# Cross-attention stage of a Perceiver layer on one core: score groups in pairs, Strassen's blocks in three PSUM banks, C22 summed into SBUF

## The chip, the core and the metric

The kernel runs on one core of one Trainium2 chip. The metric is the device time of one execution in microseconds. Before the change the median of three runs is 1519.84 us (1518.81 to 1520.62).

## The reference, cut to what matters

One layer: cross-attention of 256 latent rows over 25088 context rows, then self-attention with a bias, then a mixture of experts. The change touches the first part alone:

```python
# Q = layernorm(x), 256 x 512; K = V = ctx, 25088 x 512; 8 heads of 64
q = proj(Q, Wq, bq)
k = proj(K, Wk, bk)
v = proj(V, Wv, bv)
scores = jnp.einsum('bhqd,bhkd->bhqk', q, k) / jnp.sqrt(jnp.float32(DK))
attn = jax.nn.softmax(scores, axis=-1)
out = jnp.einsum('bhqk,bhkd->bhqd', attn, v)
```

All inputs are float32.

## The kernel before, in words

Every matmul operand is a float32 number split into a high and a low float16 part (the high part is a rounded copy, made by ScalarE; the low part is the rest, made by VectorE or GpSimd), and every product is three matmuls: high x high, low x high, high x low.

The context is read in 49 chunks of 512 rows (NCH = 49, LAST = 48). For each chunk the kernel computes K (phase h = 0) and V (phase h = 1), each as a 2 x 2 block product with seven block products in place of eight (Strassen's scheme in Winograd's form). One of these is a "unit": twelve matmuls of 128 x 128 by 256 columns. A unit writes half a bank twice, that is one bank of ps_proj. The four result blocks are C11 = M1 + M2, C12, C21 and C22. They come about so:

- M1 is built in bank 0. ScalarE copies it (seed) into the bank of role 1, and M6 adds to it there. M2 adds to bank 0: C11.
- M5 is built in a bank of its own (role 3, bank 3). ScalarE copies it to SBUF (copy_m5, tile m5_f).
- VectorE writes role 1 plus m5_f into the bank of role 2 (add_u4); M7 then adds to role 1, M3 to role 2: C12.
- VectorE writes role 1 plus m5_f into bank 3 (add_c22): C22. Then M4 adds to role 1: C21.

Roles 1 and 2 use banks 1 and 2 and change places between the phases. Each result block is split into parts by ScalarE (block_highs) and VectorE (block_lows), always in the order C11, C22, C12, C21; C21 comes at the head of the next phase. The semaphore block_low counts four of them per phase.

While the units of chunk c + 1 run, the same step c works on chunk c's attention: four groups of two heads. For each group TensorE computes scores (two heads in the two halves of 64 rows of the array, twelve matmuls, two banks of ps_s), VectorE finds the maxima (cmax, then nmax), ScalarE the exponentials (exps, tile prob, with four accumulator reads) and the high part (p_highs), VectorE the low part (p_lows), SyncE turns both by a DMA transpose into pt_s, and TensorE multiplies with V (weigh, 24 matmuls of 64 columns into ps_o) two groups later. VectorE adds the result to o_acc (add_o). GpSimd makes sums and low parts of the context two chunks ahead (ctx_sums, ctx_lows), rescales o_acc (rescale) and computes the change of the maxima (step_max); ScalarE turns that into alphas.

The order of the work is written out by hand, one list per engine (`step(c, odd)` in each engine's block), and the engines meet in semaphores. TensorE's list of a phase before: M1, scores, M5, M6, weigh, M2, scores, M7, M3, weigh, M4. Its waits that the change touches, of unit() at L1602 ff.:

```python
if m == M1:
    pe.wait_ge(block_low, 4 * g - 3)
elif m == M5:
    pe.wait_ge(block_low, 4 * g - 2 + (2 if isinstance(k, int) and g == 2 else 0))
elif m == M6:
    pe.wait_ge(seeded, g - 1)
elif m == M7:
    pe.wait_ge(u4_done, g - 1)
elif m == M4:
    pe.wait_ge(c22_done, g - 1)
```

Here g = 2k + h numbers the phases by the chunk k whose blocks are built; the lows of phase g - 1 bring block_low to 4g. So M1 waits for C11's low of the phase before, M5 for C22's.

## Time and profile before

| | us |
|---|---|
| median of 3 runs | 1519.84 |
| the profiled execution | 1517.86 |
| its span | 1516.1 |
| TensorE busy | 1452.8 (96%) |
| VectorE busy | 1298.2 (86%) |
| ScalarE busy | 1254.2 (83%) |
| GpSimd busy | 951.0 (63%) |

The profiled execution's own time is 1.76 us above its span; the median of the three runs is 1.98 above the profiled execution. The cross stage fills the span from about 10 to 1264 us. Busy time of TensorE is modelled from pipelined matmuls; the start of each is measured.

### The profile page before, as it was taken

What the parts mean: (1) busy time and instruction counts of PE and PEld (TensorE: products, weight loads), DVE (VectorE), ACT (ScalarE), POOL (GpSimd) and SP (SyncE); (2) the same over time, 40 slices, a digit from 0 to 9 for tenths busy, and PEclk for the clock granted to TensorE, in tenths of its full rate; (3) what the DMA queues carried; (4) which work ended last, traced back from release to release, by engine and by line L of the source; (5) the groups of instructions that cost most, each with busy time, mean ns of one, the idle gap of its engine ahead of it and who ended that gap; (6) DMA issues with size and microseconds to landing.
All of it is one profiled execution on the core that took longest, in us unless ns stands there. A gap on an engine that the chain in (4) does not pass through costs nothing.

```text
span 1516.1 us, 47982 instructions
## 1 busy us (share of the span) xinstructions
PE 1452.8 (96%) x17942; PEld 1206.2 (80%) x17942; DVE 1298.2 (86%) x1768; ACT 1254.2 (83%) x3039; POOL 951.0 (63%) x980
## 2 busy tenths in 40 slices
PE   6999999999999999999999999999999887599999
PEld 5788888888888888888888888888888764377776
DVE  6788989888888888898888888888889887788995
ACT  4788888888888888888888888888988875666883
POOL 6586877778687878787777878787878522500000
PEclk9999999999999999999999999999999998699999
DMA  4357555565656565655556565656566578766991
GB/s 187 71 110 143 115 135 133 122 138 117 143 113 139 111 143 112 139 119 134 135 116 143 113 145 111 138 111 145 112 137 130 116 154 223 175 232 241 337 329 46
DMA packets 460175, 220.40 MB, mean 145 GB/s; under 512 B 433856, under 2 KB 440000, under 8 KB 453328
## 3 DMA queue, kind: packets, MB, share of 16 engines
q1 hardware_dynamic: 459680, 218.22, 59.6%
q10 hardware_dynamic: 432, 1.32, 0.3%
q8 instruction: 43, 0.70, 0.2%
q14 instruction: 20, 0.16, 0.0%
HBM read 111.96 MB, written 0.56 MB: 74 GB/s over the span
## 4 chain that ended last, share of the span: by engine, by line
PE 85%; DVE 6%; DMA 3%; ACT 2%; POOL 2%; issue 1%; SPq 0%; DVEq 0%; ACTq 0%; POOLq 0%
PE ps_proj L1626 55%; PE ps_s L1676 9%; PE ps_o L1694 8%; PE ps_proj L1895 6%; PE ps_o L1911 3%; DMA pt_s<-p_s 2%; DVE wsp L1375 2%; PE ps_proj L1655 1%; POOL ctx_s L580 1%; DVE cmax L1163 1%; DVE p_s L1176 1%; PE ps_proj L1911 1%; DMA ctx_f<-ctxt_dram 1%; ACT prob L815 0%; PE ps_o L1596 0%
## 5 line engine op out<-in xcount | busy, mean ns | idle before, releaser
L1626 PE MATMUL ps_proj<-ctx_s,wk_s 128*128 128x256 f16 x4032 | 480.6, 273 | 3.9 <-ACT ps_proj L769 3.6
L1626 PE MATMUL ps_proj<-wv_s,ctx_s 128*128 128x256 f16 x4032 | 480.6, 273 | 1.5 <-ACT ps_proj L771 1.5
L580 POOL TENSOR_TENSOR ctx_s<-t_f,ctx_s 128x512 f16<-128x512 f32 x192 | 265.0, 1390 | 279.9 <-ACT ctx_s L717 279.9
L1626 PEld LDWEIGHTS ps_proj<-ctx_s,wk_s 128*128 128x128 f16 x4032 | 379.9, 98 | 66.4 <-issue 24.3
L1626 PEld LDWEIGHTS ps_proj<-wv_s,ctx_s 128*128 128x128 f16 x4032 | 379.9, 98 | 63.4 <-issue 11.4
L815 ACT ACTIVATE prob<-ps_s,nmax 128x256 f32<-128x256 f32 x776 | 357.1, 476 | 8.3 <-DVE nmax L1170 8.1
L1163 DVE TENSOR_REDUCE cmax<-ps_s 128x4 f32<-128x1024 f32 x194 | 237.5, 1224 | 123.9 <-PE ps_s L1676 123.9
L1176 DVE SCALAR_TENSOR_TENSOR p_s<-prob,p_s 128x1024 f16<-128x1024 f32 x196 | 320.3, 1634 | 0.7 <-ACT p_s L826 0.7
L580 POOL TENSOR_TENSOR ctx_s<-ctx_f,ctx_s 128x512 f16<-128x512 f32 x144 | 215.7, 1498 | 10.3 <-ACT ctx_s L712 5.4
L826 ACT ACTIVATE p_s<-prob 128x1024 f16<-128x1024 f32 x196 | 206.6, 1054 | 6.7
L1694 PE MATMUL ps_o<-v_s,pt_s 128*128 128x64 f16 x4704 | 171.6, 194 | 15.2 <-DMA pt_s<-p_s 15.2
L1694 PEld LDWEIGHTS ps_o<-v_s,pt_s 128*128 128x128 f16 x4704 | 165.2, 99 | 23.0 <-DMA pt_s<-p_s 17.8
L1676 PE MATMUL ps_s<-k_s,q_s 64*128 64x256 f16 x2328 | 160.7, 271 | 2.7 <-ACT prob L815 2.6
L815 ACT ACTIVATION_READ_ACCUMULATOR prob<-ps_s,nmax 128x1 f32 x776 | 161.6, 208 | 0.0
L1676 PEld LDWEIGHTS ps_s<-k_s,q_s 64*128 64x128 f16 x2328 | 97.5, 94 | 52.9 <-issue 39.1
L1185 DVE TENSOR_TENSOR v_s<-ps_proj,v_s 128x512 f16<-128x512 f32 x192 | 127.5, 686 | 11.4 <-ACT v_s L791 7.9
L1375 DVE SCALAR_TENSOR_TENSOR wsp<-wst,wsp 128x1024 f16<-128x1024 f32 x95 | 116.9, 1240 | 9.7 <-ACT wsp L947 9.4
L791 ACT ACTIVATE v_s<-ps_proj 128x512 f16<-128x512 f32 x192 | 108.9, 600 | 16.4 <-PE ps_proj L1626 16.4
L566 POOL TENSOR_TENSOR t_f<-ctx_f,t_f 128x512 f32<-128x512 f32 x48 | 104.8, 2184 | 0.0
L622 POOL TENSOR_TENSOR o_acc<-o_acc,alpha 128x512 f32<-128x512 f32 x98 | 103.0, 1051 | 0.0
L717 ACT ACTIVATE ctx_s<-t_f 128x1024 f16<-128x1024 f32 x96 | 100.6, 1048 | 0.1
L947 ACT ACTIVATE wsp<-wst 128x1024 f16<-128x1024 f32 x96 | 99.3, 1046 | 0.0
(235 smaller groups left out, 1800.4 us busy)
## 6 DMA issues: line engine op xcount, KB each, us to landing
ctx_f<-ctxt_dram SPq DMA_DIRECT2D x48, 1024.0 KB, 5.4
wst<-w_dram SPq DMA_DIRECT2D x96, 512.0 KB, 5.5
pt_s<-p_s SPq DMA_TRANSPOSE x408, 3.1
tisa<-tisa_scores SPq DMA_DIRECT2D x12, 256.0 KB, 5.7
w_in_f<-w_in_dram SPq DMA_DIRECT2D x2, 1024.0 KB, 6.2
w_f<-wk_dram SPq DMA_DIRECT2D x2, 512.0 KB, 6.4
ctx_f<-ctxt_dram SPq DMA_DIRECT2D x2, 512.0 KB, 7.8
w_f<-wv_dram SPq DMA_DIRECT2D x1, 1024.0 KB, 11.3
```

Of the source, the lines that this page charges most:

```text
L566: pool.tensor_tensor(out=t2, in0=b22, in1=t1, op=ALU.subtract).then_inc(t_sum, 1)
L580: pool.tensor_tensor(out=low[:, n, :, :], in0=sources[n], in1=high[:, n, :, :], op=ALU.subtract).then_inc(ctx_low, 1)
L791: ins = act.activation(out_v(0, odd, i, j), ps, ACT.Copy)
L815: ins = act.activation(prob[:, g % 2, (2 * b + r) * HC:(2 * b + r + 1) * HC], score_bank(c, g, b)[:, r * HC:(r + 1) * HC], ACT.Exp, bias=n ...
L826: act.activation(p_s[:, g % 2, 0, :], prob[:, g % 2, :], ACT.Copy, scale=P_SCALE).then_inc(p_high, 1)
L1163: dve.tensor_reduce(cmax[:, g % 2, :], ps.rearrange("p b (r k) -> p (b r) k", r=2), AX, ALU.max).then_inc(cmax_done, 1)
L1176: dve.scalar_tensor_tensor(out=p_s[:, g % 2, 1, :], in0=prob[:, g % 2, :], scalar=P_SCALE, in1=p_s[:, g % 2, 0, :], op0=ALU.mult, op1=ALU. ...
L1185: ins = dve.tensor_tensor(out_v(1, odd, i, j), ps, out_v(0, odd, i, j), ALU.subtract)
L1375: dve.scalar_tensor_tensor(out=weights(1, j)[:, n, :], in0=wst[:, j % 4, n, :], scalar=FW_SCALE, in1=weights(0, j)[:, n, :], op0=ALU.mult, ...
L1626: ins = pe.matmul(ps_proj[:, bank(h, role), sub * QUARTER:(sub + 1) * QUARTER], lhsT, rhs, start=(fresh and sub == 0 and t == 0 and i == 0 ...
L1676: ins = pe.matmul(score_bank(c, g, head)[:, r * HC:(r + 1) * HC], q_s[a][rows, g, r * P:(r + 1) * P], k_s[odd][b][rows, g, r * HC:(r + 1) ...
L1694: ins = pe.matmul(ps_o[:, vg // 2, col:col + DK], pt_s[:, vg, a, 4 * head + tile, :], v_s[vodd][b][:, tile, u * DK:(u + 1) * DK], start=(i ...
```

## The change

- Scores of groups 2h and 2h + 1 run back to back in each phase: the even group in ps_s, the odd one in ps_o. They wait once, for both exps of the phase before.
- The output of weigh goes to one bank, ps_proj bank 3, for both halves. weigh of an even group waits for add_o of the half before.
- M5 takes role 2, so the units use banks 0 to 2. M5 waits for block_low 4g, C21's low of the phase before, in place of 4g - 2.
- add_c22 writes the new SBUF tile c22_f, and both parts of C22 are made from it.
- ScalarE's, VectorE's and TensorE's lists of a phase are put in another order: p_highs and p_lows of the odd group move from the next phase into their own; alphas, the seed and ctx_highs come before the copy of M5; ctx_highs is cut in two, and its second part, sum_highs, stands between p_highs of the even group and exps of the odd one.
- The last step uses three pairs of banks for its scores and its own order.

The diff, cut to its core:

```diff
-        def score_bank(c, g, head):
-            return ps_proj[:, head, :] if isinstance(c, int) and c == LAST and g % 2 else ps_s[:, head, :]
+        def score_banks(c, g):
+            if isinstance(c, int) and c == LAST and g >= 2:
+                return (ps_proj[:, 0:2, :], ps_s[:, :, :])[g - 2]
+            return (ps_s[:, :, :], ps_o[:, :, :])[g % 2]
+        def out_bank(c, half):
+            return ps_o[:, 0, :] if isinstance(c, int) and c == LAST and half else ps_proj[:, 3, :]
...
-        M1, M5, M6, M2, M7, M3, M4 = (0, 0, 0), (3, 3, 3), (4, 4, 1), (1, 1, 0), (5, 5, 1), (6, 2, 2), (2, 6, 1)
+        M1, M5, M6, M2, M7, M3, M4 = (0, 0, 0), (3, 3, 2), (4, 4, 1), (1, 1, 0), (5, 5, 1), (6, 2, 2), (2, 6, 1)
...
-            return (0, (1, 2)[h], (2, 1)[h], 3)[role]
+            return (0, (1, 2)[h], (2, 1)[h])[role]
...
+            def sum_highs(k, odd, half):
                 act.wait_ge(t_sum, 4 * k - 1 + half)
                 act.activation(ctx_s[odd][0][:, 3 + 2 * half:5 + 2 * half, :, :], t_f[:, 2 * half:2 * half + 2, :, :],
                                ACT.Copy).then_inc(t_high, 1)
...
-                g, ps = 2 * k + h, half_bank(bank(h, role))
+                g, ps = 2 * k + h, c22_f[:, :, :] if which == C22 else half_bank(bank(h, role))
...  (ScalarE, step)
-                    if strassen:
-                        seed(c + 1, h)
-                    pc, pg = back(c, 2 * h, 1)
-                    if exists(pc, 0):
-                        p_highs(pc, pg)
                     if exists(c, -1) and h == 0:
                         alphas(c - 1, 1)
                     if exists(c, 0) and h == 1:
                         alphas(c, 0)
                     if strassen:
+                        seed(c + 1, h)
+                    if exists(c, 2):
+                        ctx_highs(c + 2, odd, h)
+                    if strassen:
                         copy_m5(c + 1, h)
                     if exists(c, 0):
                         exps(c, 2 * h, odd)
+                        p_highs(c, 2 * h)
+                    if exists(c, 2):
+                        sum_highs(c + 2, odd, h)
                     if exists(c, 0):
-                        p_highs(c, 2 * h)
+                        exps(c, 2 * h + 1, odd)
                     if strassen:
                         block_highs(c + 1, h, C11, 1 - odd)
-                    if exists(c, 2):
-                        ctx_highs(c + 2, odd, h)
                     if exists(c, 0):
-                        exps(c, 2 * h + 1, odd)
+                        p_highs(c, 2 * h + 1)
                     if strassen:
                         for which in (C22, C12):
                             block_highs(c + 1, h, which, 1 - odd)
...  (VectorE)
-                dve.tensor_tensor(half_bank(bank(h, 3)), half_bank(bank(h, 1)), m5_f[:, :, :], ALU.add).then_inc(c22_done, 1)
+                dve.tensor_tensor(c22_f[:, :, :], half_bank(bank(h, 1)), m5_f[:, :, :], ALU.add).then_inc(c22_done, 1)
...
-                    if exists(c, 0):
-                        maxima(c, 2 * h, odd)
-                    pc, pg = back(c, 2 * h, 1)
-                    if exists(pc, 0):
-                        p_lows(pc, pg)
-                    if strassen:
-                        add_u4(c + 1, h)
                     if exists(c, -1):
                         add_o(c - 1, h)
                     if exists(c, 0):
+                        maxima(c, 2 * h, odd)
                         maxima(c, 2 * h + 1, odd)
+                    if strassen:
+                        add_u4(c + 1, h)
+                    if exists(c, 0):
+                        p_lows(c, 2 * h)
                     if strassen:
                         add_c22(c + 1, h)
                         block_lows(c + 1, h, C11, 1 - odd)
                     if exists(c, 0):
-                        p_lows(c, 2 * h)
+                        p_lows(c, 2 * h + 1)
                     if strassen:
                         for which in (C22, C12):
                             block_lows(c + 1, h, which, 1 - odd)
...  (TensorE)
                 elif m == M5:
-                    pe.wait_ge(block_low, 4 * g - 2 + (2 if isinstance(k, int) and g == 2 else 0))
+                    pe.wait_ge(block_low, 4 * g)
...
                 if g == 0:
-                    pe.wait_ge(block_low, 8 * c + 4)
+                    pe.wait_ge(block_low, 8 if isinstance(c, int) and c == 0 else 8 * c + 4)
...
-                elif g >= 1 or after(c, -1):
+                elif g % 2 == 0 and (g or after(c, -1)):
                     pe.wait_ge(exp_done, NG * c + g)
...
-                if vg % 2 == 0 and after(vc, -1):
-                    pe.wait_ge(added, 2 * vc + vg // 2 - 1)
+                if isinstance(vc, int) and vc == LAST and vg == 2:
+                    pe.wait_ge(exp_done, NG * LAST + 2)
+                elif vg % 2 == 0 and (vg or after(vc, -1)):
+                    pe.wait_ge(added, 2 * vc + vg // 2)
...
-                    for half, before, between, behind in ((0, (M1,), (M5, M6), (M2,)), (1, (), (M7, M3), (M4,))):
-                        g = 2 * h + half
-                        units(*before)
-                        if exists(c, 0):
-                            scores(c, g, odd)
-                        units(*between)
-                        vc, vg = back(c, g, PV_LAG)
+                    def weighted(half):
+                        vc, vg = back(c, 2 * h + half, PV_LAG)
                         if exists(vc, 0):
-                            weigh(vc, vg, odd if g >= PV_LAG else 1 - odd)
-                        units(*behind)
+                            weigh(vc, vg, odd if 2 * h + half >= PV_LAG else 1 - odd)
+                    units(M1)
+                    if exists(c, 0):
+                        scores(c, 2 * h, odd)
+                        scores(c, 2 * h + 1, odd)
+                    units(M5, M6)
+                    weighted(0)
+                    units(M2)
+                    weighted(1)
+                    units(M7, M3, M4)
```

## Rows read from the trace of the kernel before

**Rows 1.** The page: busy time of each engine, and the chain by engine.

```profile
PE 1452.8 (96%) x17942; PEld 1206.2 (80%) x17942; DVE 1298.2 (86%) x1768; ACT 1254.2 (83%) x3039; POOL 951.0 (63%) x980
...
PE 85%; DVE 6%; DMA 3%; ACT 2%; POOL 2%; issue 1%; SPq 0%; DVEq 0%; ACTq 0%; POOLq 0%
```

**Rows 2.** Timeline of TensorE, one chunk: start us, length us, engine, line, operation, tiles.

```profile
616.28 1.47 PE L1626 MATMUL ps_proj<-ctx_s,wk_s 128*128 128x256 f16 x12
617.68 0.83 PE L1676 MATMUL ps_s<-k_s,q_s 64*128 64x256 f16 x12
618.45 2.79 PE L1626 MATMUL ps_proj<-ctx_s,wk_s 128*128 128x256 f16 x24
621.08 0.86 PE L1694 MATMUL ps_o<-v_s,pt_s 128*128 128x64 f16 x24
...
630.75 2.79 PE L1626 MATMUL ps_proj<-wv_s,ctx_s 128*128 128x256 f16 x24
...
640.89 1.47 PE L1626 MATMUL ps_proj<-ctx_s,wk_s 128*128 128x256 f16 x12
```

**Rows 3.** Timeline of ScalarE, K phase; idle time before in brackets; m_f is m5_f.

```profile
617.87 0.81 ACT L769 ACTIVATE ps_proj<-ps_proj,bk_s 128x256 f32<-128x256 f32 x2 [0.80 <-DVE v_s L1185]
...
620.04 0.60 ACT L780 ACTIVATE m_f<-ps_proj 128x512 f32<-128x512 f32 x1 [0.29 <-PE ps_proj L1626]
...
622.52 1.06 ACT L826 ACTIVATE p_s<-prob 128x1024 f16<-128x1024 f32 x1
623.48 0.82 ACT L794 ACTIVATE k_s<-ps_proj,bk_s 128x256 f16<-128x256 f32 x2
624.19 1.05 ACT L712 ACTIVATE ctx_s<-ctx_f 128x1024 f16<-128x1024 f32 x1
625.14 1.05 ACT L717 ACTIVATE ctx_s<-t_f 128x1024 f16<-128x1024 f32 x1
626.09 0.47 ACT L815 ACTIVATE prob<-ps_s,nmax 128x256 f32<-128x256 f32 x1
...
627.88 1.60 ACT L796 ACTIVATE k_s<-ps_proj 128x512 f16<-128x512 f32 x3
```

**Rows 4.** Timeline of ScalarE, V phase.

```profile
632.27 0.60 ACT L780 ACTIVATE m_f<-ps_proj 128x512 f32<-128x512 f32 x1 [0.46 <-PE ps_proj L1626]
...
634.81 1.06 ACT L826 ACTIVATE p_s<-prob 128x1024 f16<-128x1024 f32 x1
635.77 0.58 ACT L791 ACTIVATE v_s<-ps_proj 128x512 f16<-128x512 f32 x1
636.25 0.62 ACT L715 ACTIVATE ctx_s<-ctx_f 128x512 f16<-128x512 f32 x1
```

**Rows 5.** Timeline of VectorE, the same chunk.

```profile
617.11 0.69 DVE L1185 TENSOR_TENSOR v_s<-ps_proj,v_s 128x512 f16<-128x512 f32 x1 [0.16 <-ACT v_s L791]
...
620.36 2.37 DVE L1176 SCALAR_TENSOR_TENSOR p_s<-prob,p_s 128x1024 f16<-128x1024 f32 x1
...
624.05 1.23 DVE L1163 TENSOR_REDUCE cmax<-ps_s 128x4 f32<-128x1024 f32 x1
625.31 0.17 DVE L1170 SCALAR_TENSOR_TENSOR nmax<-cmax,nmax 128x4 f32<-128x4 f32 x1
...
628.62 1.87 DVE L1191 TENSOR_TENSOR k_s<-ps_proj,k_s 128x512 f16<-128x512 f32 x3
```

**Rows 6.** The page, p_lows: instructions, busy us, mean ns of one, idle before.

```profile
L1176 DVE SCALAR_TENSOR_TENSOR p_s<-prob,p_s 128x1024 f16<-128x1024 f32 x196 | 320.3, 1634 | 0.7 <-ACT p_s L826 0.7
```

**Rows 7.** By line, p_lows and V lows: ns min/median/max, first and last start.

```profile
L1176 DVE SCALAR_TENSOR_TENSOR p_s<-prob,p_s x171: 1203/1219/2376, 202.1 to 1249.2; 128x1024 f16<-128x1024 f32 x171
...
L1185 DVE TENSOR_TENSOR v_s<-ps_proj,v_s x168: 678/683/693, 220.1 to 1239.4; 128x512 f16<-128x512 f32 x168
```

**Rows 8.** Timeline of GpSimd beside p_lows.

```profile
620.39 1.27 POOL L564 TENSOR_TENSOR t_f<-ctx_f 128x512 f32<-128x512 f32 x1
```

**Rows 9.** The page: the DMA transposes, us to landing.

```profile
pt_s<-p_s SPq DMA_TRANSPOSE x408, 3.1
```

More of the change, by code:

```diff
@@ L201, in layer @@
         m5_f = sb("m5_f", [P, 2, QUARTER], F32, cross)
+        c22_f = sb("c22_f", [P, 2, QUARTER], F32, cross)
         q_s = [sb(f"q_s{k}", [P, NG, T], F16, cross) for k in range(2)]
@@ L399, in out_v @@
             return v_s[odd][kk][:, 2 * j:2 * j + 2, i * QUARTER:(i + 1) * QUARTER]
-        C11, C22, C12, C21 = (0, 0, 0), (3, 1, 1), (2, 0, 1), (1, 1, 0)
+        C11, C22, C12, C21 = (0, 0, 0), (None, 1, 1), (2, 0, 1), (1, 1, 0)
         def half_bank(n):
@@ L1181, in block_lows @@
                 role, i, j = which
-                g, ps = 2 * k + h, half_bank(bank(h, role))
+                g, ps = 2 * k + h, c22_f[:, :, :] if which == C22 else half_bank(bank(h, role))
                 dve.wait_ge(block_high, 4 * g + 1 + (C11, C22, C12, C21).index(which))
@@ L1218, in add_o @@
                 acc = o_acc[:, half, :, :, :].rearrange("p u r d -> p (u r d)")
-                dve.tensor_tensor(acc, acc, ps_o[:, half, :], ALU.add).then_inc(added, 1)
+                dve.tensor_tensor(acc, acc, out_bank(c, half), ALU.add).then_inc(added, 1)
             def by_rows(t, half):
@@ L1295, in last_step @@
                 block_lows(LAST, 1, C21, LAST % 2)
+                add_o(LAST - 1, 0)
                 maxima(LAST, 0, LAST % 2)
-                p_lows(LAST - 1, 3)
                 maxima(LAST, 1, LAST % 2)
-                add_o(LAST - 1, 0)
                 tisa_scores()
                 p_lows(LAST, 0)
+                maxima(LAST, 2, LAST % 2)
                 add_o(LAST - 1, 1)
-                maxima(LAST, 2, LAST % 2)
                 p_lows(LAST, 1)
@@ L1675, in scores @@
                             rows = slice(DK * head, DK * head + DK)
-                            ins = pe.matmul(score_bank(c, g, head)[:, r * HC:(r + 1) * HC], q_s[a][rows, g, r * P:(r + 1) * P],
+                            ins = pe.matmul(score_banks(c, g)[:, head, r * HC:(r + 1) * HC], q_s[a][rows, g, r * P:(r + 1) * P],
                                             k_s[odd][b][rows, g, r * HC:(r + 1) * HC], start=(n == 0), stop=(n == 2))
@@ L1729, in last_step @@
                 scores(LAST, 1, odd)
+                scores(LAST, 2, odd)
                 tisa_scores()
                 weigh(LAST - 1, 2, 1 - odd)
-                scores(LAST, 2, odd)
                 weigh(LAST - 1, 3, 1 - odd)
```

26 lines of the change are left out of this document (13 added, 13 removed).

## The prediction

> **What bounds the kernel now.** I read the page first: TensorE is busy 96% of the span, and the chain of waits is 85% TensorE [rows 1]. The reader should see one engine filled and two (VectorE 86%, ScalarE 83%) close behind. Then TensorE's timeline in the middle of the cross stage [rows 2]: every run of instructions begins where the one before it ends, no idle time is printed behind any row, and one chunk takes 640.89 - 616.28 = 24.61 us, half of it per phase (K blocks, then V blocks). So matmul issue sets the pace there, and anything that shortens TensorE's list could shorten the kernel. The timeline also shows where TensorE loses time without idling. Two units in a run take 621.08 - 618.45 = 2.63, 1.315 each, 0.109 per matmul; the unit ahead of a group of scores takes 617.68 - 616.28 = 1.40, so 0.085 more. The twelve score matmuls use 64 rows each and run two at a time, six times 0.109 = 0.65, but take 618.45 - 617.68 = 0.77. Going into the 64-row form and back out costs 0.085 + 0.12 = 0.20 us per group of scores, four times a chunk.
>
> Last I read ScalarE's and VectorE's timelines of the same chunk [rows 3 to 5] for what they do between two uses of one PSUM bank, since the change gives fewer banks to Strassen's blocks.
>
> **The change part by part.**
>
> *Scores of two groups back to back.* Two of four round trips between the forms go: 2 x 0.20 = 0.40 us a chunk. If TensorE stayed the bound a chunk would take 24.21.
>
> *TensorE's list of a phase.* It becomes M1, scores, scores, M5, M6, weigh, M2, weigh, M7, M3, M4, with the same count of matmuls.
>
> *Three banks.* M5 now goes to the bank in which the phase before built C21, so its wait moves from the low part of C22 to the low part of C21, the last of the four. That is the edit I price highest, because of what stands ahead of it. On VectorE, C21's low follows the lows of C12, C22 and p_lows of the second group; that p_lows waits for p_highs of the second group on ScalarE; and there the order is now copy of M5, exps, p_highs, sum_highs, exps, high of C11, p_highs. The old order left p_highs and p_lows of the second group to the next phase, behind the seed and the first maxima; now they are in the way of C21. The copy of M5 in turn waits for M5. So there is a loop: M5 of one phase to M5 of the next. Its length, first for the K phase:
> - M5 starts 618.45, the copy of it 620.04: 1.59 [rows 2, 3]
> - copy, then exps with their accumulator reads, to p_highs: 622.52 - 620.04 = 2.48
> - p_highs to the next instruction: 623.48 - 622.52 = 0.96
> - sum_highs (L717): 626.09 - 625.14 = 0.95
> - the second exps: 627.88 - 626.09 = 1.79
> - high of C11, two pieces: 624.19 - 623.48 = 0.71 [all rows 3]
> - second p_highs, to its end: 0.96 and 0.10 of overlap, 1.06; over to VectorE 0.04 (an estimate, half of the next message)
> - p_lows with no delay: 1.22, less 0.08 by which the next one overlaps it: 1.14 (an estimate) [rows 7]
> - lows of C22, C12, C21: 1.87 for three in a row [rows 5]
> - back to TensorE: 0.07, as from VectorE's 617.11 + 0.69 to the seed at 617.87 [rows 3, 5]
>
> Sum 12.66. In the V phase M5 to copy is 632.27 - 630.75 = 1.52, copy to p_highs 634.81 - 632.27 = 2.54 and high of C11 636.25 - 635.77 = 0.48 [rows 2, 4], the rest the same: 12.42. Together 25.08 a chunk with nothing delayed, against 24.61 now and 24.21 for TensorE alone. The loop, not TensorE, sets the pace.
>
> *Delays on the loop.* p_lows is not always 1.22: the fastest is 1.203, the median 1.219, the longest 2.376 [rows 7], the mean 1.634 [rows 6]. Its inputs both lie in SBUF. At 620.36 it took 2.37 while GpSimd ran an instruction from 620.39 to 621.66 [rows 5, 8]: it ended about 1.1 after that one did, so it stood still until then. The lows of V blocks, one input in PSUM, run 678 to 693 ns in all 168 cases beside the same GpSimd work [rows 7]. The reader sees two kinds of VectorE instruction: one that waits for a running GpSimd instruction and one that doesn't. The mean delay of p_lows is 1.634 - 1.219 = 0.415, and both loops of a chunk have one: +0.83.
>
> *C22 in SBUF.* Its low now reads c22_f and the high part, both SBUF. The trace of before has no such instruction of this size. From below it costs nothing more (0.62, as the PSUM lows); from above it waits like the worst p_lows, +1.16. I take the mean delay of p_lows, 0.415, the nearest row in kind: twice a chunk, +0.83. It follows p_lows directly, and a GpSimd instruction that p_lows held up goes in between, so nothing is gained from below. add_c22 itself keeps a PSUM input and its 0.70.
>
> The Trainium skill (SBUF — State Buffer, "SBUF: two separate sides") says that VectorE and GpSimd share one port pair as an exclusive lock, taken by a VectorE instruction in a two-port mode or with two SBUF inputs, for its whole length. By that rule the move of C22 works against this kernel; without it the sum would be 0.83 a chunk less, 38 us in all. The trace agrees with it in p_lows.
>
> *Sum.* 25.08 + 0.83 + 0.83 = 26.74 a chunk, 2.13 more than 24.61. Strassen's blocks run beside scores in 48 steps (chunks 0 to 47); the first two fill the pipeline, so 46 count: 46 x 2.13 = 98.0. The profiled execution took 1517.86 (span 1516.1): 1615.9. The median of the runs is 1519.84, 1.98 above the profiled one: 1617.8, say 1618.
>
> *What costs nothing.* The second way into exps, C21's low, then add_o (0.6, a PSUM input like the lows), first maxima (1.26 to the next) and nmax (0.17) [rows 5]: 2.0 to exps against 2.1 through M5 and its copy; if nmax meets GpSimd it is up to 0.9 late (in the upper end of the range). M1 waits for C11's low, which lies before p_lows of the second group; M5 waits longer anyway. M7 waits for add_u4, M4 for add_c22 with only M3 (1.31) between M7 and M4, against M3 and a weigh (2.0) before: sum of messages and 0.70 is about 1.0, so it holds while VectorE is free; if p_lows of the first group is running, M4 is up to 0.5 late, but that is TensorE's time, of which 26.74 - 24.21 = 2.53 a chunk is now free. ScalarE's other work fits in: from the end of the second p_highs to the next copy lie 0.04 + 1.14 + 1.87 + 0.07 + 1.59 = 4.7 us undelayed, and the highs of C22, C12 and C21 (0.5 each), alphas, the seed and ctx_highs need 3.4 of them; alphas also wait for GpSimd's rescale and dmax, behind three low parts: four instructions of 1.27 [rows 8], about 5.1 us behind sum_highs; the seed that follows alphas is wanted some 7.5 behind it. Transposes on SyncE: the second group's low part is ready 2 us before the next M5, its transpose takes 3.1 [rows 9], and the weigh that reads it comes two units, a weigh and M2 later, 4.6 behind M5: 3.5 us of cover, so a transfer that lands 2 late is still hidden. The load of the next chunk sits behind group 0's transposes as before. One output bank: weigh of an even group waits for add_o of the half before, which now comes right behind C21's low, 4 us ahead of it. First and last step: the pair of scores in step 0 waits for all of chunk 0's V lows, and the last step runs three groups of scores at once; I put both at 0 within 3 us.
>
> **The rivals.**
> 1. *The locks slip aside.* If p_lows and C22's low meet no GpSimd instruction, a chunk is 25.08: 46 x 0.47 = 22, so 1541. For it: the schedule repeats every chunk, so one instruction meets the same neighbour each time, and the median p_lows is undelayed [rows 7]. Against it: behind every sum_highs GpSimd runs two or three low parts and the rescale, 3.8 to 5.1 us at 1.27 each [rows 8], and p_lows of the second group comes 1.79 + 0.6 + 1.1 = 3.5 behind sum_highs, into the middle of it. Half of the delays give 25.9 and 1579.
> 2. *More waits than I count.* nmax delayed, or alphas waiting for dmax in one phase, 1.2 a chunk more: 27.9, so 1673.
> 3. *TensorE stays the bound*, the other side. The place is the last wait before M5: if C21's low is done when the second group of scores ends, the 0.40 is all that is left: 1519.8 - 46 x 0.40 = 1501. It decides at a loop of 24.21 / 2 = 12.10 us; the rows give 12.66 and 12.42 undelayed, so 0.3 to 0.6 of what I put on the loop would have to lie beside it. The Trainium skill (TensorEngine Tiling (Array Packing), "Key Properties") says that changing the tiling mode drains TensorE; by that rule this edit can only help, and the 0.20 per group in the trace agrees. It says nothing of the banks paid for it.
> 4. *Both cancel*: the loop at 12.3, 1520.
>
> **How the numbers follow.** Forecast with delays in both phases (26.3 to 27.4 a chunk, 1597 to 1648): 0.61. Half of them, 1560 to 1597: 0.17. Undelayed, 1530 to 1560: 0.07. More waits, above 1648: 0.09. TensorE the bound: 0.04; cancelled: 0.02. The range 1560 to 1660 leaves out the last two, the undelayed case and half of the upper one: 0.18. About 0.2% is what a measurement of this kernel can tell from no change. Faster 0.04, same 0.02, slower 0.94.
>
> **What would show it.** In the profile after: a chunk of about 26.7 on TensorE's timeline, idle time in front of M5 in each phase, 1.0 to 1.5 us, released by the low of C21 (k_s or v_s on VectorE); one 1.40 unit per phase instead of two, and the pair of scores at about 1.4; p_lows of the second group directly ahead of the lows of C22, C12, C21; C22's low longer than 0.68 in part of the cases, C12's never; ScalarE waiting for M5 before its copy. I am wrong on the loop if M5 starts without idle time, wrong on the lock if C22's low is always 0.68, and wrong on the size if the idle time before other units (M1, M7, M4) is larger than before M5.

## The result, and the profile after

The changed kernel takes 1588.25 us (median of 4 runs, 1585.88 to 1588.87), beside 1519.32 (4 runs) for the kernel before. The ratio is 1.0452 (1.0433 to 1.047): slower by 4.5%. The forecast was 1618 with a range of 1560 to 1660. Direction and mechanism came out as forecast. The size did not: of the 98 us put on the change, 71 came.

The profiled execution is the 1588.87 one, with a span of 1587.1. From its page: the busy time of each engine, the chain by engine, and the two groups of units (idle time before them at the end of the line):

```profile
PE 1451.0 (91%) x17942; PEld 1222.5 (77%) x17942; DVE 1256.4 (79%) x1768; ACT 1253.2 (79%) x3039; POOL 968.0 (61%) x980
...
issue 37%; POOL 33%; PE 15%; DVE 7%; ACT 5%; DMA 2%; POOLq 1%; SPq 0%; ACTq 0%; DVEq 0%
...
L1629 PE MATMUL ps_proj<-wv_s,ctx_s 128*128 128x256 f16 x4032 | 474.1, 273 | 53.2 <-DVE k_s L1194 27.0
L1629 PE MATMUL ps_proj<-ctx_s,wk_s 128*128 128x256 f16 x4032 | 474.1, 273 | 29.3 <-DVE v_s L1191 26.1
```

TensorE does the same 17942 matmuls in the same busy time as in [rows 1], but fills 91% of the span where it filled 96%. The chain was 85% TensorE; now TensorE has 15% of it, GpSimd 33%, and 37% is "issue", time in which the engine on the chain waited for nothing that the profile shows. This line does not name the loop, and read alone it would point at GpSimd; how much of the time is GpSimd's is what experiment 3 measures. The units stood idle for 53.2 + 29.3 = 82.5 us. Its timeline in the middle of the stage, and two rows near its end:

```profile
647.15 1.47 PE L1629 MATMUL ps_proj<-ctx_s,wk_s 128*128 128x256 f16 x12
648.56 0.83 PE L1680 MATMUL ps_s<-k_s,q_s 64*128 64x256 f16 x12
...
650.53 2.78 PE L1629 MATMUL ps_proj<-ctx_s,wk_s 128*128 128x256 f16 x24 [0.49 <-DVE v_s L1191]
...
660.48 1.48 PE L1629 MATMUL ps_proj<-wv_s,ctx_s 128*128 128x256 f16 x12 [0.53 <-DVE k_s L1194]
...
663.89 2.79 PE L1629 MATMUL ps_proj<-wv_s,ctx_s 128*128 128x256 f16 x24 [0.51 <-DVE k_s L1197]
...
673.16 1.47 PE L1629 MATMUL ps_proj<-ctx_s,wk_s 128*128 128x256 f16 x12
...
1239.35 4.26 PE L1629 MATMUL ps_proj<-wv_s,ctx_s 128*128 128x256 f16 x24 [4.10 <-DVE k_s L1197]
...
1256.93 5.28 PE L1629 MATMUL ps_proj<-ctx_s,wk_s 128*128 128x256 f16 x24 [3.94 <-DVE v_s L1191]
```

One chunk is 673.16 - 647.15 = 26.01 us, where [rows 2] gave 24.61. M5, the row of 24 behind each pair of scores, has idle time in front of it in both phases, and what ends it is the low of C21 (v_s or k_s). From M5 to M5 it is 663.89 - 650.53 = 13.36 us in the K phase and 676.54 - 663.89 = 12.65 in the V phase (the next M5 starts at 676.54). Without its idle time M5 could begin at 650.53 - 0.49 = 650.04 at the latest (the end of the scores is modelled), so the pair of scores takes at most 650.04 - 648.56 = 1.48 with the way back to the 128-row form; in experiment 7, where nothing is waited for, it is 652.87 - 651.45 = 1.42. Two groups cost 2 x 0.77 + 0.085 = 1.62 before, so the pairing does give something, and the loop eats it.

VectorE around the end of that loop, V phase and then K phase:

```profile
647.22 1.35 DVE L1182 SCALAR_TENSOR_TENSOR p_s<-prob,p_s 128x1024 f16<-128x1024 f32 x1 [0.25 <-ACT p_s L833]
648.50 0.68 DVE L1191 TENSOR_TENSOR v_s<-c_f,v_s 128x512 f16<-128x512 f32 x1
...
652.20 0.69 DVE L1176 SCALAR_TENSOR_TENSOR nmax<-cmax,nmax 128x4 f32<-128x4 f32 x1
...
660.49 1.53 DVE L1182 SCALAR_TENSOR_TENSOR p_s<-prob,p_s 128x1024 f16<-128x1024 f32 x1
661.95 0.69 DVE L1197 TENSOR_TENSOR k_s<-c_f,k_s 128x512 f16<-128x512 f32 x1
```

ScalarE in the K phase, the loop's steps in order:

```profile
650.44 0.21 ACT L812 ACTIVATE alpha<-dmax 128x8 f32<-128x8 f32 x1 [1.76 <-POOL dmax L639]
...
652.29 0.59 ACT L787 ACTIVATE m_f<-ps_proj 128x512 f32<-128x512 f32 x1
...
654.96 1.06 ACT L833 ACTIVATE p_s<-prob 128x1024 f16<-128x1024 f32 x1
655.93 1.04 ACT L724 ACTIVATE ctx_s<-t_f 128x1024 f16<-128x1024 f32 x1
...
658.67 0.84 ACT L801 ACTIVATE k_s<-ps_proj,bk_s 128x256 f16<-128x256 f32 x2
659.38 1.08 ACT L833 ACTIVATE p_s<-prob 128x1024 f16<-128x1024 f32 x1
```

GpSimd beside it:

```profile
646.34 1.15 POOL L584 TENSOR_TENSOR ctx_s<-t_f,ctx_s 128x512 f16<-128x512 f32 x1
647.46 1.18 POOL L624 TENSOR_TENSOR l_acc<-l_acc,alpha 128x8 f32<-128x8 f32 x1
648.60 1.48 POOL L626 TENSOR_TENSOR o_acc<-o_acc,alpha 128x512 f32<-128x512 f32 x1
650.05 0.20 POOL L629 TENSOR_TENSOR l_acc<-l_acc,lsum 128x8 f32<-128x8 f32 x1
...
659.91 1.03 POOL L626 TENSOR_TENSOR o_acc<-o_acc,alpha 128x512 f32<-128x512 f32 x1
660.91 1.18 POOL L629 TENSOR_TENSOR l_acc<-l_acc,lsum 128x8 f32<-128x8 f32 x1
662.05 0.65 POOL L639 TENSOR_TENSOR dmax<-nmax 128x8 f32<-128x8 f32 x1
```

And p_lows on the page (it had a mean of 1634 ns in [rows 6]), then the two lows of C22 by line over 200 to 1280 us (ns min/median/max):

```profile
L1182 DVE SCALAR_TENSOR_TENSOR p_s<-prob,p_s 128x1024 f16<-128x1024 f32 x196 | 275.3, 1405 | 119.9 <-ACT p_s L833 116.5
```

```profile
L1191 DVE TENSOR_TENSOR v_s<-c_f,v_s x41: 682/684/687, 206.5 to 1251.2; 128x512 f16<-128x512 f32 x41
L1197 DVE TENSOR_TENSOR k_s<-c_f,k_s x41: 677/684/685, 219.9 to 1270.2; 128x512 f16<-128x512 f32 x41
```

Read VectorE's rows, GpSimd's and the lows of C22 together. In the V phase p_lows is issued at 647.22 while GpSimd is in a low part that ends at 647.49; it takes 1.35, 0.13 over its undelayed 1.22. In the K phase it is issued at 660.49 while GpSimd rescales o_acc until 660.94; it takes 1.53. Then it is the other way round: the short l_acc that GpSimd wants next (0.20 at 650.05) takes 1.18 in both phases, because p_lows runs. The lows of C22 come straight behind p_lows and take 0.68 to 0.69 in all 82 cases: here it is GpSimd that stands still, o_acc for 1.48 and not 1.03, dmax for 0.65 and not 0.20.

**Where the 71 us are.** The profiled executions differ by 71.0. From the first M1 of a K phase to the last (47 intervals), chunks 5 to 45 take 26.00 where they took 24.61: 41 x 1.39 = 57.0. The first four take 107.18 where they took 103.11: 4.1. The last two take 62.20 where they took 55.15: 7.1; those are the two rows at 1239 and 1256 above. These rows are also longer than the 2.79 of their kind, by 1.47 and 2.49: behind 4.10 and 3.94 us of idle time the granted clock of TensorE is 0.64 over the first and 0.50 (1.2 GHz) over the second, where it is 1.00 in the middle of the stage. So 4.0 of the 7.1 are the clock. The first M1 comes 0.3 later, and the stretch behind the last M1 is 2.4 longer. By the prediction's own count (46 x 1.39 = 64) the regular part is 64 and the ends are 7.

### The profile page after: what moved, and what is told of

Same layout as the page of the kernel before. It is cut to its first block, busy times and chain, and to the rows that moved or that the text cites. A ratio compares the mean times of both kernels' runs of the same rounds, so it can differ in the third digit from the quotient of the medians.

```text
span 1587.1 us, 47836 instructions
## 1 busy us (share of the span) xinstructions
PE 1451.0 (91%) x17942; PEld 1222.5 (77%) x17942; DVE 1256.4 (79%) x1768; ACT 1253.2 (79%) x3039; POOL 968.0 (61%) x980
## 4 chain that ended last, share of the span: by engine, by line
issue 37%; POOL 33%; PE 15%; DVE 7%; ACT 5%; DMA 2%; POOLq 1%; SPq 0%; ACTq 0%; DVEq 0%
POOL ctx_s L584 16%; PE ps_proj L1905 6%; POOL l_acc L629 4%; POOL l_acc L624 3%; POOL t_f L570 3%; POOL t_f L567 3%; PE ps_o L1921 3%; ACT prob L822 2%; POOL dmax L639 2%; DVE wsp L1378 2%; PE ps_proj L1658 1%; DMA pt_s<-p_s 1%; ACT p_s L833 1%; PE ps_proj L1629 1%; DVE p_s L1182 1%
## 5 line engine op out<-in xcount | busy, mean ns | idle before, releaser
L1629 PE MATMUL ps_proj<-wv_s,ctx_s 128*128 128x256 f16 x4032 | 474.1, 273 | 53.2 <-DVE k_s L1194 27.0
L1629 PE MATMUL ps_proj<-ctx_s,wk_s 128*128 128x256 f16 x4032 | 474.1, 273 | 29.3 <-DVE v_s L1191 26.1
L1182 DVE SCALAR_TENSOR_TENSOR p_s<-prob,p_s 128x1024 f16<-128x1024 f32 x196 | 275.3, 1405 | 119.9 <-ACT p_s L833 116.5
L822 ACT ACTIVATE prob<-ps_s,nmax 128x256 f32<-128x256 f32 x392 | 180.0, 475 | 8.7 <-DVE nmax L1176 3.9
L1700 PE MATMUL ps_proj<-v_s,pt_s 128*128 128x64 f16 x4656 | 168.9, 194 | 8.6 <-DMA pt_s<-p_s 8.6
L822 ACT ACTIVATE prob<-ps_o,nmax 128x256 f32<-128x256 f32 x388 | 176.6, 464 | 0.0
L1700 PEld LDWEIGHTS ps_proj<-v_s,pt_s 128*128 128x128 f16 x4656 | 163.4, 98 | 14.5 <-DMA pt_s<-p_s 9.3
L584 POOL TENSOR_TENSOR ctx_s<-ctx_f,ctx_s 128x512 f16<-128x512 f32 x144 | 166.7, 1158 | 2.9 <-ACT ctx_s L716 2.9
L1378 DVE SCALAR_TENSOR_TENSOR wsp<-wst,wsp 128x1024 f16<-128x1024 f32 x95 | 116.9, 1239 | 9.1 <-ACT wsp L954 8.7
L1169 DVE TENSOR_REDUCE cmax<-ps_s 128x4 f32<-128x1024 f32 x98 | 118.8, 1212 | 0.0
L1169 DVE TENSOR_REDUCE cmax<-ps_o 128x4 f32<-128x1024 f32 x97 | 118.1, 1217 | 0.0
L787 ACT ACTIVATE m_f<-ps_proj 128x512 f32<-128x512 f32 x96 | 57.2, 596 | 55.8 <-PE ps_proj L1629 55.8
L1194 DVE SCALAR_TENSOR_TENSOR k_s<-ps_proj,bk_s,k_s 128x256 f16<-128x256 f32 x96 | 42.0, 480 | 62.5 <-ACT k_s L801 62.4
```

The costliest lines, as they stand in the source:

```text
L584: pool.tensor_tensor(out=low[:, n, :, :], in0=sources[n], in1=high[:, n, :, :], op=ALU.subtract).then_inc(ctx_low, 1)
L822: ins = act.activation(prob[:, g % 2, (2 * b + r) * HC:(2 * b + r + 1) * HC], score_banks(c, g)[:, b, r * HC:(r + 1) * HC], ACT.Exp, bias= ...
L1169: dve.tensor_reduce(cmax[:, g % 2, :], score_banks(c, g).rearrange("p b (r k) -> p (b r) k", r=2), AX, ALU.max).then_inc(cmax_done, 1)
L1182: dve.scalar_tensor_tensor(out=p_s[:, g % 2, 1, :], in0=prob[:, g % 2, :], scalar=P_SCALE, in1=p_s[:, g % 2, 0, :], op0=ALU.mult, op1=ALU. ...
L1378: dve.scalar_tensor_tensor(out=weights(1, j)[:, n, :], in0=wst[:, j % 4, n, :], scalar=FW_SCALE, in1=weights(0, j)[:, n, :], op0=ALU.mult, ...
L1629: ins = pe.matmul(ps_proj[:, bank(h, role), sub * QUARTER:(sub + 1) * QUARTER], lhsT, rhs, start=(fresh and sub == 0 and t == 0 and i == 0 ...
```

## The experiments

Experiments 1 to 4 are compared with 1517.21 us for the kernel before, experiments 5 to 8 with 1520.11. "A chunk" is from M1 to M1 of the K phases in the middle of the stage.

**1. odd_back: p_highs and p_lows of the second group back into the next phase.** Three banks, C22 in SBUF and the pairs stay.

```diff
  (ScalarE, step, behind the seed)
+                    pc, pg = back(c, 2 * h, 1)
+                    if exists(pc, 0):
+                        p_highs(pc, pg)
...
-                    if exists(c, 0):
-                        p_highs(c, 2 * h + 1)
  (VectorE, step)
                         maxima(c, 2 * h, odd)
+                    if exists(pc, 0):
+                        p_lows(pc, pg)
...
-                    if exists(c, 0):
-                        p_lows(c, 2 * h + 1)
```

> The changed kernel with p_highs and p_lows of the odd group put back where they were (behind the seed on ScalarE, behind the first maxima on VectorE); three banks, C22 in SBUF and the pair of scores stay. Loop theory: C21's low no longer stands behind p_highs (1.06), the message (0.04) and p_lows (1.14 and its delays), so the loop from M5 to M5 falls from 13.0 on average to about 10.8 and TensorE becomes the bound: 24.21 a chunk, 1499 to 1505 us, no idle time before M5. Rival (three banks or the lock cost the time whatever the order): at least 25.5 a chunk, 1560 or more.

Measured: 1643.31 (1640.99 to 1646.57), ratio 1.0834 (1.0812 to 1.0856). Missed by 140 us, and not for the reason that was tested. TensorE's timeline, then VectorE's:

```profile
607.19 0.87 PE L1704 MATMUL ps_proj<-v_s,pt_s 128*128 128x64 f16 x24 [2.04 <-DMA pt_s<-p_s]
...
614.65 2.79 PE L1633 MATMUL ps_proj<-wv_s,ctx_s 128*128 128x256 f16 x24
...
619.87 0.87 PE L1704 MATMUL ps_proj<-v_s,pt_s 128*128 128x64 f16 x24 [0.42 <-DMA pt_s<-p_s]
```

```profile
601.65 2.37 DVE L1183 SCALAR_TENSOR_TENSOR p_s<-prob,p_s 128x1024 f16<-128x1024 f32 x1
```

M5 (614.65) has no idle time in front of it, in either phase: with the two instructions out of the way the loop is gone. But the new order of TensorE wants the second group's weigh only one unit behind the first's, and p_lows, which again meets GpSimd (2.37), ends at 604.0; its transpose lands some 3 us later, while weigh could have begun 2.04 us earlier. A chunk takes 25.9 to 28.7. In the 8 chunks of the middle above 28 us the mean granted clock of TensorE is 0.94, in all others there 1.00: behind some of the waits it falls (0.70 over 714.65 to 720.25, behind 1.91 us of idle time and one weigh). That confirms what the loop ran through, and the early place of p_highs and p_lows turns out to be what the pair of weighs needs. In this TensorE order the loop is the price of transposes that are in time. The time alone would fit the rival of this run as well (three banks cost time in any order, 1560 or more); what speaks against the rival is M5 without idle time here, and experiments 6 and 7, which keep the three banks at 25.19 and 24.19 a chunk. C22's low is delayed here: 1.15 to 1.17 us in the V phase, 0.69 to 1.50 in the K phase.

**2. low_behind_c21: only p_lows moved, behind C21's low.**

```diff
  (VectorE, step, behind C21's low, ahead of add_o)
+                    pc, pg = back(c, 2 * h, 1)
+                    if exists(pc, 0):
+                        p_lows(pc, pg)
...  (behind C11's low)
-                    if exists(c, 0):
-                        p_lows(c, 2 * h + 1)
```

> The changed kernel with p_lows of the odd group alone moved, from before the low of C22 to behind the low of C21 on VectorE; ScalarE's list stays. Loop theory: the loop through M5 loses p_lows and now goes through ScalarE's highs of C22, C12 and C21 (0.5 + 0.5 + 0.6), undelayed 12.66 - 0.83 = 11.8 and 11.6, under TensorE's 12.1; but p_lows stays on the other way to exps (p_highs, p_lows, add_o, maxima, nmax), which is then 2.48 + 0.96 + 0.95 + 1.79 + 0.71 + 1.06 + 0.04 + 1.14 + 0.61 + 1.26 + 0.21 less the copy 0.5 = 12.7. So 25.1 to 25.9 a chunk, 1540 to 1580, with TensorE's idle time no longer ended by the low of C21. Rival (only the order ahead of C21 counts): 24.2 a chunk, 1500.

Measured: 1696.89 (1691.84 to 1699.82), ratio 1.1174 (1.1146 to 1.1203), 28.2 to 28.4 a chunk. Missed by over 110 us. The waits (us in total, times, longest), ScalarE's timeline, and VectorE's:

```profile
ACT prob L822 <- DVE nmax L1176: 91.2, 74, 1.5
```

```profile
646.14 0.60 ACT L787 ACTIVATE m_f<-ps_proj 128x512 f32<-128x512 f32 x1 [0.51 <-PE ps_proj L1631]
648.24 0.47 ACT L822 ACTIVATE prob<-ps_s,nmax 128x256 f32<-128x256 f32 x1 [1.50 <-DVE nmax L1176]
```

```profile
641.75 1.46 DVE L1191 TENSOR_TENSOR v_s<-c_f,v_s 128x512 f16<-128x512 f32 x1 [0.77 <-ACT v_s L798]
...
644.33 1.41 DVE L1182 SCALAR_TENSOR_TENSOR p_s<-prob,p_s 128x1024 f16<-128x1024 f32 x1
```

There are two ways from C21's low into the exponentials: M5 and its copy, or add_o, the maxima and nmax. The prediction had them at 2.1 and 2.0 us. With p_lows in the second one it is 1.33 longer in the K phase (644.33 to 645.66) and 1.13 in the V phase, and the exponentials wait for nmax (1.50 and 0.92), after the copy of M5 is long done. The expectation named this second way and mis-sized it twice. Its terms add up to 10.7, not to the 12.7 it gives. And they leave out what now stands between the second p_highs and p_lows: the high of C22, and the lows of C22, C12 and C21. From the start of C22's high to p_lows are 644.33 - 641.07 = 3.26 us in the V phase, and 3.35 in the K phase. With that the sum is 14.0; measured are 14.1 to 14.2 a phase. M5 also still waits for C21's low (0.62 and 0.43), which the expectation had ruled out: with p_lows gone from before it, C21's low still comes behind C22's high and the delayed C22's low. C22's low, here behind an idle VectorE, takes 1.46 in the V phase and 1.54 in the K phase.

**3. short_pool: GpSimd's part in the delays.** Its sums of context blocks and low parts are cut to 16 elements per row in the loop.

```diff
+                w = QUARTER if isinstance(k, int) else 8
+                b11, b12, b21, b22 = (b[:, :, 0:w] for b in (b11, b12, b21, b22))
...
-                    pool.tensor_tensor(out=low[:, n, :, :], in0=sources[n], in1=high[:, n, :, :],
+                    pool.tensor_tensor(out=low[:, n, :, 0:w], in0=sources[n][:, :, 0:w], in1=high[:, n, :, 0:w],
```

> The changed kernel with GpSimd's sums and low parts of the context cut from 512 to 16 elements a partition for the chunks inside the loop, so most of that arithmetic is left out; every other instruction and all waits stay. Loop theory: the delays go (p_lows 1.22, nmax 0.17, dmax early), the bare loop stays: 25.08 a chunk, about 1545, idle time before M5 in each phase. Rival (GpSimd's locks are the whole cost): 24.2 a chunk, 1505.

Measured: 1554.75 (1553.91 to 1556.36), ratio 1.0246 (1.0229 to 1.0263). TensorE, then VectorE:

```profile
647.65 2.79 PE L1632 MATMUL ps_proj<-wv_s,ctx_s 128*128 128x256 f16 x24 [0.20 <-DVE k_s L1200]
...
660.18 2.78 PE L1632 MATMUL ps_proj<-ctx_s,wk_s 128*128 128x256 f16 x24 [0.36 <-DVE v_s L1194]
```

```profile
644.57 1.23 DVE L1185 SCALAR_TENSOR_TENSOR p_s<-prob,p_s 128x1024 f16<-128x1024 f32 x1
645.71 0.68 DVE L1200 TENSOR_TENSOR k_s<-c_f,k_s 128x512 f16<-128x512 f32 x1
```

This is nearly the bare loop: 25.16 to 25.27 a chunk, where the prediction's sum without delays was 25.08, and M5 still waits for C21's low. The time is 10 us above the expected one, 6 of it from 0.14 a chunk and the rest at the ends, which the expectation left out. From p_lows to the next instruction are 645.71 - 644.57 = 1.14, the estimate of the prediction. So in the changed kernel the loop costs about 25.22 - 24.61 = 0.6 a chunk over before, and GpSimd 26.00 - 25.22 = 0.78 more. The prediction had 0.47 and 1.66.

**4. before_m5_wait: the kernel before, with the later wait alone.** M5 of the kernel before waits for C21's low though it does not need to.

```diff
-                    pe.wait_ge(block_low, 4 * g - 2 + (2 if isinstance(k, int) and g == 2 else 0))
+                    pe.wait_ge(block_low, 4 * g)
```

> The kernel before with one edit: M5 waits for C21's low of the phase before in place of C22's. Loop theory: there C21's low ends about 1.5 us into the phase and M5 starts 2.2 into it, so 24.61 a chunk and 1519 to 1521. Rival (the wait itself, needed for three banks, costs the time): 0.5 us or more a phase, above 1560.

Measured: 1526.54 (1525.15 to 1527.09), ratio 1.0061 (1.0044 to 1.0078). A chunk is 24.61, as before, with no idle time on TensorE. The later wait costs nothing in the middle of the stage; it takes the new order of ScalarE and VectorE to make a loop of it. But the run is 9 us longer, and the expectation missed that. TensorE near the end of the stage:

```profile
1177.78 4.39 PE L1626 MATMUL ps_proj<-wv_s,ctx_s 128*128 128x256 f16 x24 [3.17 <-DVE k_s L1191]
...
1196.08 4.21 PE L1626 MATMUL ps_proj<-ctx_s,wk_s 128*128 128x256 f16 x19 [4.33 <-DVE v_s L1185]
```

In the last two chunks VectorE and ScalarE also prepare the next stage, C21's low comes late, and M5 is what waits: the two chunks take 30.63 + 32.48 = 63.1, 8.0 more than before. The changed kernel's last two take 62.2, 7.1 more than before. So the wait alone is enough for what the changed kernel loses at that end. Here too a part of it is the clock: behind the idle time it is 0.62 over the row at 1177.78 and 0.50 over the one at 1196.08, which together are 4.1 us longer than two of 2.79 (the second is cut by the window above; its 24 matmuls take 5.28).

**5. weigh_back: odd_back, with the second weigh between M3 and M4**, where it was before the change.

```diff
                     units(M2)
+                    units(M7, M3)
                     weighted(1)
-                    units(M7, M3, M4)
+                    units(M4)
```

> odd_back with one more edit: the second weigh goes back to its old place, between M3 and M4. In odd_back TensorE waited 2.04 us in the K phase and 0.42 in the V phase for the transposes of the odd group, and M5 not at all. With the weigh 2.6 us later those waits go, but in the K phase M7 would then start about 605.0 on odd_back's clock and add_u4 ends at 607.1, behind p_lows and the second maxima. So the K phase stays about 2 us long and the V phase falls to 12.1: 26.2 a chunk, about 1600. Rival (the transposes were the only wait left): 24.2 to 24.6, 1500 to 1520.

Measured: 1636.97 (1623.42 to 1640.3), ratio 1.078 (1.0762 to 1.0798), 25.4 to 28.6 a chunk. Some 37 us above what was expected. The transposes are no longer waited for, and next in line is add_u4, as expected. The wait (us in total, times, longest), and TensorE's timeline:

```profile
PE ps_proj L1633 <- DVE ps_proj L1208: 76.7, 39, 2.6
```

```profile
655.15 4.45 PE L1633 MATMUL ps_proj<-ctx_s,wk_s 128*128 128x256 f16 x24 [2.40 <-DVE ps_proj L1208]
```

M7 waits 2.4 us for add_u4, which on VectorE stands behind both maxima and a p_lows of 2.37 us between them. The row behind the wait shows what the expectation left out: M7 and M3 take 4.45 where they take 2.79 elsewhere. The granted clock of TensorE over 656.5 to 658.5 is 0.50, the 1.2 GHz level, where it was 1.00 up to the idle time. The 12 chunks of the middle with such a fall (mean clock 0.94) take 28.4 to 28.6. Others wait as long (2.64 before 683.80), keep the clock at 1.00 and take 26.7 to 27.0. Over the whole run 13 rows are 1.3 to 1.7 longer, some 20 us in all, of the 23 by which the profiled execution (1623.42) is above what was expected.

**6. u4_back: weigh_back, with add_u4 ahead of the second maxima.**

```diff
-                    if exists(c, 0):
-                        maxima(c, 2 * h + 1, odd)
                     if strassen:
                         add_u4(c + 1, h)
                     if exists(c, 0):
+                        maxima(c, 2 * h + 1, odd)
+                    if exists(c, 0):
                         p_lows(c, 2 * h)
```

> weigh_back with add_u4 moved ahead of the second maxima on VectorE, where it stood before the change. add_u4 then ends at 604.8 on odd_back's clock, before M7's start at 605.0. Loop theory: every long way between two uses of a bank is then shorter than TensorE's list, 24.2 to 25.0 a chunk depending on GpSimd's delays, 1505 to 1545. Rival (three banks cost time in any order): above 25.5, 1565 or more.

Measured: 1545.54 (1544.34 to 1546.92), ratio 1.0171 (1.0154 to 1.0188), 25.19 a chunk, just above the upper end of what was expected (25.0 and 1545): one step moved, 91 us gained. ScalarE's largest wait (us in total, times, longest), and TensorE:

```profile
ACT alpha L812 <- POOL dmax L639: 100.3, 81, 1.5
```

```profile
643.66 1.49 PE L1633 MATMUL ps_proj<-wv_s,ctx_s 128*128 128x256 f16 x12 [0.30 <-DVE k_s L1195]
...
663.76 2.78 PE L1633 MATMUL ps_proj<-ctx_s,wk_s 128*128 128x256 f16 x24 [0.36 <-DVE ps_proj L1208]
```

M1 of the V phase now waits for C11's low, which hangs on the high of C11 behind both exponentials; M7 of the K phase still waits for add_u4, behind a p_lows of 2.37; and ScalarE starts each phase by waiting for dmax.

**7. tuned: u4_back with those waits taken off.** ScalarE puts the seed ahead of alphas, and C11's high ahead of the second exponentials; VectorE puts add_c22 ahead of p_lows; TensorE does M2 ahead of the first weigh.

```diff
  (ScalarE; order of a phase: C21's high, seed, alphas, ctx_highs, p_highs of the group before, sum_highs, copy of M5)
                         exps(c, 2 * h, odd)
-                        p_highs(c, 2 * h)
-                    if exists(c, 2):
-                        sum_highs(c + 2, odd, h)
-                    if exists(c, 0):
-                        exps(c, 2 * h + 1, odd)
                     if strassen:
                         block_highs(c + 1, h, C11, 1 - odd)
+                    if exists(c, 0):
+                        p_highs(c, 2 * h)
+                        exps(c, 2 * h + 1, odd)
  (VectorE)
+                    if strassen:
+                        add_c22(c + 1, h)
                     if exists(c, 0):
                         p_lows(c, 2 * h)
                     if strassen:
-                        add_c22(c + 1, h)
                         block_lows(c + 1, h, C11, 1 - odd)
  (TensorE)
-                    units(M5, M6)
+                    units(M5, M6, M2)
                     weighted(0)
-                    units(M2)
```

> u4_back with its lists ordered by the same arithmetic: ScalarE C21, seed, alphas, ctx_highs, p_highs of the odd group before, sum_highs, copy of M5, exps, C11, p_highs, exps, C22, C12 (sum_highs 5 us earlier, so GpSimd's low parts and alphas are early and run while VectorE reads PSUM); VectorE add_c22 ahead of p_lows; TensorE M2 ahead of the first weigh. Loop theory: TensorE is the bound, 24.1 to 24.3 a chunk against 24.61, and 1500 to 1510 us: faster than the kernel before by 0.7 to 1.3%. Rival (delays by GpSimd decide): 24.6 to 25.3, 1520 to 1555.

Measured: 1501.45 (1500.99 to 1506.48), ratio 0.9878 (0.9861 to 0.9894): 1.2% faster than the kernel before, 87 us faster than the changed one, with its three banks, its pairs and C22 in SBUF all kept. TensorE, then the low of C22 in the V phase on VectorE:

```profile
650.04 1.47 PE L1634 MATMUL ps_proj<-wv_s,ctx_s 128*128 128x256 f16 x12
651.45 0.83 PE L1685 MATMUL ps_s<-k_s,q_s 64*128 64x256 f16 x12
...
652.87 4.10 PE L1634 MATMUL ps_proj<-wv_s,ctx_s 128*128 128x256 f16 x36
```

```profile
661.39 1.16 DVE L1192 TENSOR_TENSOR v_s<-c_f,v_s 128x512 f16<-128x512 f32 x1
```

No row of a chunk has idle time; a chunk is 24.19, and the prediction had 24.21 for TensorE alone. The delays by GpSimd are still there (1.16), but off the path. Of the rate, 46 x 0.42 = 19 us of gain are made. The ends leave something lying: in the profiled execution, at 1506.48 the slowest of the four, the first chunk takes 32.3, with 6.4 us of waiting for add_u4 and the clock at 0.64 over the row behind it, where it took 26.0 before. Which of the three engines' edits gave how much was not separated.

**8. sum_highs_late: the changed kernel, with sum_highs behind the second p_highs.** This takes one term out of the loop.

```diff
                         p_highs(c, 2 * h)
-                    if exists(c, 2):
-                        sum_highs(c + 2, odd, h)
...
                         p_highs(c, 2 * h + 1)
+                    if exists(c, 2):
+                        sum_highs(c + 2, odd, h)
```

> The changed kernel with sum_highs moved from before the second exps to behind the second p_highs. The loop from M5 to M5 gets 0.95 shorter. But GpSimd gets the sums 3.6 us later and with them its low parts, rescale and dmax, for which alphas wait ahead of the seed: sum_highs 1.0, two or three low parts, rescale and dmax 3.8 to 5.1, alphas 0.1, seed 0.7, ctx_highs 0.95, copy 0.5, exps to p_highs 2.0, p_highs 0.96, exps 1.8, C11 0.7, p_highs 0.96 make 13.5 to 14.8. Loop theory with that second loop: 27 to 29.5 a chunk, 1630 to 1750, ScalarE waiting for dmax. Rival (only what stands ahead of C21's low counts): 24.2 to 24.5, 1505 to 1520.

Measured: 1730.11 (a single run, beside 1520.11), 29.1 to 29.3 a chunk, as expected. The waits:

```profile
ACT alpha L812 <- POOL dmax L639: 251.0, 72, 4.0
...
PE ps_proj L1629 <- ACT ps_proj L776: 67.7, 36, 1.9
```

A term of 0.95 leaves the first loop and a second one closes: sum_highs, GpSimd's low parts behind it, rescale, dmax, alphas, the seed behind alphas, M6. ScalarE stands up to 4.0 us before alphas. One in-order queue is a member of every loop that passes through its engine, so a step is only cheap to move in the direction in which nobody waits for what it feeds.

## Why the prediction was right in kind and too high in size

**The loop.** Its terms, undelayed as predicted against the changed kernel's rows (differences of starts above; in the V phase from the same steps between 663.89 and 676.54):

| step | K predicted | K after | V predicted | V after |
|---|---|---|---|---|
| M5 to its copy | 1.59 | 1.76 | 1.52 | 1.52 |
| copy to p_highs | 2.48 | 2.67 | 2.54 | 2.53 |
| p_highs, sum_highs, exps | 3.70 | 3.71 | 3.70 | 3.71 |
| high of C11 | 0.71 | 0.71 | 0.48 | 0.47 |
| second p_highs, over to p_lows | 1.10 | 1.11 | 1.10 | 1.11 |
| p_lows | 1.14 + 0.415 | 1.46 | 1.14 + 0.415 | 1.28 |
| lows of C22, C12, C21, to M5 | 1.94 + 0.415 | 1.94 | 1.94 + 0.415 | 2.03 |
| sum | 13.49 | 13.36 | 13.25 | 12.65 |

The steps that nothing delayed are within 0.02 us of their rows from the kernel before; the exception is the way back to M5 in the V phase, 0.09 longer. Adding up a cycle from the starts of the old timeline works even when the order is new, as long as the instructions are the same. Experiments 3 (loop alone) and 1 (loop undone, no wait at M5) show it by themselves; rival 3 (TensorE stays the bound) is refuted for this order and true of experiment 7. Rival 4 (both cancel) is refuted.

**The failed term: the delays on the loop**, 0.83 + 0.83 = 1.66 a chunk in the prediction. p_lows was delayed by 0.32 + 0.14 = 0.46, not 0.83. C22's low was not delayed at all: "I am wrong on the lock if C22's low is always 0.68" is what happened. In exchange, 0.17 + 0.19 + 0.09 = 0.45 came from places counted at nothing: the copy of M5 late behind alphas (which wait for dmax, which waits behind p_lows and C22's low), nmax at 0.69 in place of 0.16, and the handover in the V phase. With 0.02 of small differences that is 0.93, which is 26.01 - 25.08. So 26.74 should have been 26.0, and 46 x 0.74 = 34 us of the forecast were too much; the ends, 7 us that it left out, bring that to the 27 by which the profiled execution missed its 1615.9. That the forecast came as close as it did is partly luck: the two delays alone were 46 x 1.20 = 55 us too high, and some 28 of them were made good by terms put at nothing.

The reason is in GpSimd's rows. The prediction took the mean delay of [rows 6], made in an order where p_lows met the 1.27 us sums (620.39 in [rows 8]). In the new order the second p_lows meets the tail of a low part or of the rescale, with 0.27 and 0.45 us left to run, and behind that short l_acc instructions. A schedule that repeats has one neighbour per instruction, as rival 1 said; the prediction argued that and then used the mean all the same. Rival 1's half case (1560 to 1597, chance 0.17) is where the time fell, and not the main case (0.61). Rival 2 had its mechanism right as well: nmax was delayed and alphas waited for dmax (1.76 before 650.44), but the two cost 0.19 + 0.17 a chunk, not 1.2.

**Who waits.** In the rows the delay of a VectorE instruction with two SBUF inputs is what is left of GpSimd's running instruction, less about 0.14: p_lows had 0.27 left and was delayed 0.13 (647.22), 0.45 and 0.31 (660.49), nmax 0.67 and 0.53 (652.20, beside a sum that ends at 652.87), and in [rows 5, 8] 1.30 and 1.15. C22's low in the changed kernel has 0.14 left (648.50 against l_acc's end at 648.64) and no delay. So "a GpSimd instruction that p_lows held up goes in between" was right, but that instruction is 0.2 long. The low is of the kind that waits all the same: 1.15 to 1.17 in experiment 1 (V phase), 1.46 and 1.54 in experiment 2, while lows with a PSUM input stay at 0.67 to 0.69 in every kernel. The Trainium skill (SBUF — State Buffer, "SBUF: two separate sides") has an exclusive lock of the port pair for such instructions; the rows agree in both directions, since o_acc and dmax on GpSimd are stretched beside C22's low. The lock was read rightly, and priced by the wrong neighbour.

**The pairs.** 2 x 0.20 a chunk is confirmed by experiment 7: 24.19.

**The ends**, put at 0 within 3, cost 7. Experiment 4 has the cause of most of it: the later wait of M5 meets C21's late low in the last two chunks, and the granted clock of TensorE falls behind the wait. The prediction has no term for the clock: 4.0 us in the changed kernel, 20 in experiment 5.

**The signs named.** Idle time before M5, released by C21's low: there in both phases, but 0.5 and not 1.0 to 1.5. Idle before M1 of the V phase, released by C11's low (0.53), is as large as before M5. It was named as a sign of a wrong size, and the size was wrong. It needs care in reading: as M5 waits anyway, a phase whose M1 came 0.53 earlier would wait that much longer before M5; the chunk is set by the loop either way. C12's low never longer than 0.69: so. ScalarE waiting for M5 before its copy: only in the V phase (1.03 at 665.41); in the K phase it came late itself.

**The transposes** were predicted hidden with 3.5 us of cover, and in the changed kernel they are. Experiment 1 shows what the cover was worth.

## What to carry to other kernels

When banks get fewer, write down the cycle: from the write of a bank through every in-order queue to the wait that frees it, and compare its length with the work of the bounding engine per turn; a wait that is free in one order of the queues (24.61 in experiment 4) sets the pace in another (25.2 in experiment 3). If a change pays in a cycle, the repair is to move the steps that sit in the cycle without belonging to it, one at a time and with the waits read again after each, since each move puts another wait last: here transposes, then add_u4, then alphas and C11, and only then did the gain of the pairs appear. For contention between two engines, take the neighbour that the new order gives and not the mean of the old one.
